# Inverse roots of the head norms in the local tiles: one power instruction on GpSimd in place of two ScalarE activations and a Newton step on VectorE

## The reference, cut to what matters

```python
h = shift_token(x)
q, k, v = split(h @ wqkv)            # 8 heads of 64
q = l2norm(q) * q_scale              # l2norm(t) = t / clip(norm(t), 1e-12), per head
k = l2norm(k) * k_scale
q, k = rotary_xpos(q, k)
o = local_attention(q, k, v)         # softmax over a window of 64 tokens and itself
x = x + o @ wo
h = layernorm(shift_token(x)) ; a, g = split(h @ w1 + b1)
x = x + (a * gelu(g)) @ w2 + b2
```

## Time and profile before

| | |
|---|---|
| median of 3 runs (lowest, highest) | 409.67 us (408.95, 409.79) |
| span of the profiled execution, first to last instruction | 406.5 us |
| median less that span (what lies around the span) | 3.2 us |
| TensorE, VectorE, ScalarE, GpSimd busy | 87%, 83%, 73%, 14% |
| phase of the local tiles' queries and keys, first pair sum to last rescaling | 204.5 to 370.0 us |

### The profile page before, as it was taken

The page is one execution under the profiler, slowest core; times in us unless marked ns, Lnnn a source line. Parts: engine busy times, 40 slices in busy tenths (PEclk is TensorE's granted clock), DMA queues, the critical chain, the costliest instruction groups (busy, mean ns, idle before and its releaser), DMA issues.

```text
span 406.5 us, 10233 instructions
## 1 busy us (share of the span) xinstructions
PE 352.7 (87%) x4033; PEld 251.1 (62%) x4036; DVE 338.9 (83%) x725; ACT 295.9 (73%) x727; POOL 58.6 (14%) x45
## 2 busy tenths in 40 slices
PE   2899999999945878998798889999999999998676
PEld 1498888887731424555455556567676767676565
DVE  5989987887789889979679999989899999986343
ACT  1789999896434337776747787898989898986663
POOL 2000002000003021000023123403132323212110
PEclk9999999999985699999989999999999999999779
DMA  8800010000000000000000000000000000000001
GB/s 315 347 4 3 4 42 3 3 4 3 2 0 0 2 1 0 2 2 2 0 2 2 0 0 2 0 2 2 1 2 2 1 2 0 2 2 0 2 1 52
DMA packets 1774, 8.29 MB, mean 20 GB/s; under 512 B 192, under 2 KB 448, under 8 KB 1472
## 3 DMA queue, kind: packets, MB, share of 16 engines
q1 hardware_dynamic: 1728, 7.65, 4.8%
HBM read 7.12 MB, written 0.52 MB: 19 GB/s over the span
## 4 chain that ended last, share of the span: by engine, by line
PE 43%; DVE 29%; ACT 17%; issue 10%; DMA 1%; DVEq 0%; ACTq 0%
PE ps L252 15%; ACT PT L1525 5%; ACT blk L1411 3%; DVE PT L1232 3%; PE ps L506 3%; DVE lneg L1216 3%; PE ps L620 3%; DVE blk L1190 2%; DVE ss_floor L1200 2%; PE ps L656 2%; ACT PT L1595 2%; PE ps L379 2%; PE ps L493 2%; DVE Y L870 2%; PE ps L582 2%
## 5 line engine op out<-in xcount | busy, mean ns | idle before, releaser
L1724 POOL TENSOR_TENSOR blk<-blk 128x1024 f32<-128x1024 f32 x16 | 37.7, 2359 | 170.6 <-DVE blk L1194 170.6
L568 PE MATMUL ps<-w_f,full 128*128 128x512 f32 x96 | 48.2, 619 | 0.9 <-issue 0.9
L1525 ACT ACTIVATE PT<-ps,lneg 128x128 f32<-128x128 f32 x128 | 45.0, 377 | 5.3 <-DVE lneg L1216 5.3
L252 PEld LDWEIGHTS ps<-blk,st 128*128 128x128 bf16 x768 | 26.8, 98 | 3.8
L1045 DVE TENSOR_REDUCE mneg<-ps 128x4 bf16<-128x512 bf16 x32 | 22.0, 688 | 7.7 <-PE ps L357 7.4
L1525 ACT ACTIVATION_READ_ACCUMULATOR PT<-ps,lneg 128x1 f32 x128 | 27.9, 218 | 0.0
L252 PE MATMUL ps<-blk,rel 128*128 128x64 bf16 x768 | 27.6, 193 | 0.0
L252 PE MATMUL ps<-blk,st 128*128 128x64 bf16 x768 | 27.6, 193 | 0.0
L1582 ACT ACTIVATE PT<-ps 128x512 f32<-128x512 f32 x32 | 17.5, 595 | 13.2 <-PE ps L506 13.2
L1216 DVE TENSOR_REDUCE lneg<-ps 128x8 f32<-128x1024 f32 x16 | 19.6, 1223 | 8.6 <-PE ps L252 8.5
L1232 DVE TENSOR_TENSOR PT<-PT,lrec 128x512 f32<-128x512 f32 x32 | 25.3, 790 | 1.1
(11 more groups left out here) (234 smaller groups left out, 905.5 us busy)
## 6 DMA issues: line engine op xcount, KB each, us to landing
w_f<-f_dram SPq DMA_DIRECT2D x2, 1689.0 KB, 13.3
w_x<-l_dram SPq DMA_DIRECT2D x1, 774.0 KB, 5.9
w_f<-ffn_dram SPq DMA_DIRECT2D x1, 561.0 KB, 7.9
X<-x_dram SPq DMA_DIRECT2D x1, 512.0 KB, 3.6
ctxT<-ctxT_dram SPq DMA_DIRECT2D x1, 512.0 KB, 4.4
OT<-maskT_dram SPq DMA_DIRECT2D x1, 512.0 KB, 7.1
rest<-l_dram SPq DMA_DIRECT2D x1, 385.0 KB, 4.8
const<-const_dram SPq DMA_DIRECT2D x1, 324.0 KB, 6.3
```

The costliest lines, as they stand in the source:

```text
L252: return mm(out, l, r, start=start, stop=False, skip_group_check=True)
L568: m = mm(ps[:, c, :], hT[:, n, :], w_f[:, l, F_QKV + 512 * c:F_QKV + 512 * (c + 1)], start=True, stop=True)
L1525: e = a(S1[:, i % 2, P * k:P * (k + 1)], ps[:, 3 + c, P * j:P * (j + 1)], ACT.Exp, bias=lneg[:, i % 2, k:k + 1], accum_out=lsum[:, i % 2, ...
L1724: g_.tensor_tensor(R[:, i % 2, :], R[:, i % 2, :], T2, ALU.add).then_inc(sem("pair_sum"), 1)
```

## The change

The logarithm, the exponential and the Newton step for the head norms go. In their place GpSimd raises ss to the power -0.5 in one instruction (`tensor_tensor` with `ALU.pow`), with a tile `root_power` of exponents that is filled with -0.5 once at the start. It stands in GpSimd's program right behind each pair sum. It waits for `ss` of its tile and for the rescaling of the tile before, and signals `rate`, for which the rescaling waits. VectorE's last reduce of `sum_squares` also waits for `rate` of the tile before, which the rescaling just ahead of it in the program has waited for already.

```diff
-        lss = sb("lss", [2 * LH])
-        lr0 = sb("lr0", [2 * LH])
-        lnt = sb("lnt", [2, 2 * LH])
         lr = sb("lr", [2 * LH])
+        root_power = sb("root_power", [2 * LH])
...
                 settle()
+                if i >= 1:
+                    dve.wait_ge(sem("rate"), i)
                 v.tensor_reduce(ss[:, :], ss_floor[:, :, :], AX.X, ALU.max).then_inc(sem("ss"), 1)
 
             def unit_norm(i):
-                dve.wait_ge(sem("root"), i + 1)
+                dve.wait_ge(sem("rate"), i + 1)
                 dve.wait_ge(sem("pair_sum"), i + 1)
-                newton(ss[:, :], lr0[:, :], lnt, lr[:, :])
                 r = R[:, i % 2, :].rearrange("p (h j) -> p h j", j=LD)
...
-            def head_root(i):
-                act.wait_ge(sem("ss"), i + 1)
-                root(ss[:, :], lss[:, :], lr0[:, :], "root")
-
...
+            g_.memset(root_power[:, :], -0.5).then_inc(sem("root_power"), 1)
...
             def sum_pairs(i):
                 pool.wait_ge(sem("rotated"), i + 1)
                 g_.tensor_tensor(R[:, i % 2, :], R[:, i % 2, :], T2, ALU.add).then_inc(sem("pair_sum"), 1)
-
+                pool.wait_ge(sem("ss"), i + 1)
+                if i >= 1:
+                    pool.wait_ge(sem("rope"), i)
+                g_.tensor_tensor(lr[:, :], ss[:, :], root_power[:, :], ALU.pow).then_inc(sem("rate"), 1)
+
+            pool.wait_ge(sem("root_power"), 1)
```

More of the change, by code:

```diff
@@ L1599, in _ @@
                     take_v(0)
-            head_root(0)
             square(1)
@@ L1604, in _ @@
             take_turned_qk(0)
-            head_root(1)
             for i in range(4):
@@ L1622, in _ @@
                 take_turned_p(i)
-                head_root(i + 2)
                 if i == 3:
```

## The result

The changed kernel takes 426.22 us, the median of four runs, beside 409.31 us for the kernel before. The ratio is 1.044, with a 95% interval of 1.038 to 1.051: 4.4% slower, 17 to 18 us. The forecast was 408.3 us with a range up to 418.0; the slower side had 36%.

What follows compares the result with a forecast made beforehand. Three engines nearly full, no bound from averages; even passes ran through VectorE's chain, TensorE's 0.68 us idle per period capping gains. Gains of 2.6 us less 1.25 gave 1.35 off 409.67: 408.3 us, range 405.5 to 418.

Steps and rivals of the forecast that it cites:

- Between the ends I take 1.0 us, by the rows that do the same arithmetic now: GpSimd's power per tile: 1.0 us, from ScalarE's two activations and three VectorE instructions, together 0.94 us.
- upper end: GpSimd's power per tile: 2.4 us if a column costs 64 adds; the lower bound was 0.17 us.
- p: Duration of the 128x16 power on GpSimd behind each pair sum, shown in no row; taken as 1.0 us.
- 300.33 + p against 301.62: Even pass: the rescaling's start after the change against before, gaining 1.29 - p, at most 0.54 us.
- The meeting with the bias add: Even pass: the bias add on Z, delayed by the power, meets VectorE's rescaling, both reading two SBUF operands.
- the 0.14 us rule: Two-operand SBUF meetings: VectorE stands until about 0.14 us before the GpSimd row's end, then runs at full length.
- the second meeting: Even tile's power beside VectorE's second half of the probabilities: 0.25 us in each of five even passes, 1.25 us.
- The power is the new wait, slower: Rival: from p = 1.3 us every even pass loses; 413.8 us at 1.5, 419.5 at 2.0; 36%.
- up to 0.54 us in each even pass: Even passes: most the rescaling could gain by starting at the largest score's end, 301.08, instead of 301.62.
- the 0.9 us of tiles 7, 9 and 11 in the sum: Even-pass rescalings of these tiles: 0.3 us gained each at p = 1.0.
- the quick power's 406.3: Rival: p up to 0.6 us with reads done early, even passes at their cap, 3.4 us gained, 406.3 us; 20%.
- ScalarE's two activations were worth nothing: Removed ScalarE activations, 6.9 us of busy time over 16 tiles: counted at nothing, hidden by VectorE's chain in even passes.

Runs made afterwards that it cites:

- run 4: Kernel before plus powers and products of several widths on GpSimd in its idle time, off the path; the 16-column power took 2.90 us.
- run 2: Changed kernel with the bias add on Z ahead of the odd tile's pair sum instead of behind its power; 420.93 us, ratio 1.029.
- run 9: Changed kernel with unread matmuls put into TensorE's longest idle times, in tiles 1 to 4 and the pass of tile 14; 426.18 us, ratio 1.043.
- run 6: Kernel before with the power for tiles 6, 8, 10, 12 and 14 alone, the old way elsewhere; 408.42 us, ratio 0.999.
- run 3: Kernel before without the Newton step on the head norms, ScalarE's logarithm and exponential writing lr at once; 405.49 us, ratio 0.995.
- run 1: Changed kernel with the power replaced by an add of the same shape, place and waits; 405.59 us, ratio 0.991.
- run 7: Kernel before with the power for tiles 5, 7, 9, 11 and 13 alone, the old way elsewhere; 414.83 us, ratio 1.017.

## Why the prediction was wrong

**The step that failed** is "Between the ends I take 1.0 us, by the rows that do the same arithmetic now". The power takes 2.9 us (result, run 4), above even the 2.4 us that was named as the upper end "though it could be beyond". ScalarE's two activations and VectorE's three small rows take 0.94 us and were taken as a guide, because together they do the power's arithmetic. GpSimd takes 0.17 us for each column of it, and no row of adds or activations could price that. The range up to 418 stood on 2 us. The added duration turned a forecast gain of 1.35 us into a loss of 17 to 18.

**The wait was foreseen rightly.** With p = 2.9 the prediction's own formula, 300.33 + p against 301.62, gives 1.6 us of delay in an even pass; the period grew by 1.52. The meeting with the bias add cost 0.52 us, as the 0.14 us rule from two old rows said, and run 2 took it away. The same sums at 2.9 us, without the second meeting, give 4.8 (tiles 7, 9, 11) + 1.8 (tile 5) + 1.5 + 1.5 (13 and 15) + 1.6 (tile 1) + 0.2 (tile 2) + 3.4 (tiles 3 and 4) = 14.8 us. "The power is the new wait, slower" was this rival; its price was cut off too low.

**Two terms were put at nothing.** The third meeting, VectorE's product on `nt` beside the add of X, costs 0.5 us each in the passes of tiles 12 and 14. From tile 13's pair sum to tile 14's it takes 10.96 us in place of 8.99, so 1.97 more, the 1.5 above and this 0.5. The prediction had seen only that the second add can meet the rescaling, when the power is quick. And TensorE's lower clock behind its longer idle time costs 1.7 us in the pass of tile 14 (run 9). With these the sum is 14.8 + 1.0 + 1.7 = 17.5 us, beside 17.8 between the two spans.

**The second meeting** was taken at half its bound, 0.25 us a period. It costs nothing: VectorE's half took 0.69 us beside a running power, and run 6 has five such meetings at no cost. The Trainium skill (SBUF — State Buffer, "Who interferes with whom") has the shared ports held for the whole instruction. Here the trace differs: a power of 3.36 us, of which the first 0.45 are its own wait, held them so briefly that VectorE's next two-operand row, 0.72 us behind its start, found them free. That the power's reads are done early in it is inferred from this. Where GpSimd came second it did wait, as the Trainium skill says in that section: 3.36 - 2.91 = 0.45 us, of the 0.60 for which VectorE's first half still ran (317.60 + 1.32 against 318.32).

**The gain was mis-sized too.** The prediction gave the Newton step up to 0.54 us in each even pass, from TensorE's idle time and the chain. It was worth 0.01 there (run 3), and the idle time is no cap of its own: ScalarE's square, held by TensorE's order, tied with VectorE's chain. So the 0.9 us of tiles 7, 9 and 11 in the sum had no source. That the quick power's 406.3 came out near run 1's 405.59 is luck in part. Tiles 1 and 2 gave their 0.4 and 0.6 us in its trace (8.98 and 11.30 us to the next pair sum in place of 9.38 and 11.93) and tile 5 gave 0.3. The other 2 us lie behind tile 15's pair sum, where run 7, which is the kernel before there, is 1.1 us shorter than the profile before as well. That ScalarE's two activations were worth nothing held: run 1 takes them away beside the Newton step and is no faster in the period than run 3.

**What stays open.** The terms of 0.5 and 1.7 us outside the steady part are read from single executions, and the median of run 9 did not move. Behind the pass of tile 14, where the kernels are alike, the profiled executions differ by 1 to 3 us (from the bias add at the end of that pass to the end of the span 23.9 us before, 24.9 with the change, 22.4 in run 6), so that the sum's closeness to 17.8 is no proof of each term. Why VectorE isn't held off by a running power is inferred and not measured.

## What to carry to other kernels

An operation that no row of the profile shows has no price until it is run by itself, in an engine's idle time (run 4); a sum by the same arithmetic on other engines was wrong by three times. Before an edit is credited with what it takes off the chain that ended last, look for a second chain that ends just before it at the same wait: here 0.1 us apart, so that taking 0.62 us away won nothing and adding 0.62 cost all of it in that pass. And work given to an idle engine is free only behind the cover of its own reader: the same instruction, of 2.9 to 3.4 us, cost nothing with 4.4 us of cover and 1.5 us a period with 1.3. A lower clock too costs only where its engine is waited for: nothing in tile 1, 1.7 us in the pass of tile 14.

## What the runs showed of the hardware

A power of two tensors on GpSimd costs 0.17 us a column on 128 partitions, as much on 16, where an add costs 2.2 ns a column. It did not keep VectorE from reading two operands in SBUF 0.72 us behind its start (0.69 us, full speed), though an add or a bias add of GpSimd did, to 0.14 us before its end (the rescaling 1.75 us in place of 1.23). With idle times of 2.9 and 3.3 us TensorE's granted clock fell to 0.85 and 0.56 of a stretch, so partly to its lower level of 1.2 GHz, and eight turns took 1.97 us in place of 1.09; with matmuls in the idle time they took 1.09.
